# Distance attention worked in pairs of head groups, with three distance buffers and its loads on the sync engine

## What is computed

```python
q2 = jnp.sum(q * q, axis=-1)
k2 = jnp.sum(k * k, axis=-1)
qk = jnp.einsum('bhid,bhjd->bhij', q, k)
d2 = jnp.maximum(q2[..., :, None] + k2[..., None, :] - 2.0 * qk, 1e-12)
attn = jax.nn.softmax(-jnp.sqrt(d2), axis=-1)
out = jnp.einsum('bhij,bhjd->bhid', attn, v)
out = out.transpose(0, 2, 1, 3).reshape(B, N, D)
return out @ wo.T + bo
```

## Time and profile before

| what | us |
|---|---|
| median of 3 runs | 3940.42 (3935.94 to 3940.86) |
| the profiled execution's own time | 3938.66 |
| its span, first to last instruction | 3937.0 |
| the stage of the change: first minimum starts | 3236.41 |
| PE, DVE, ACT, POOL busy over the span | 3315.0, 3175.2, 2294.0, 1649.5 |

### The profile page before, as it was taken

The page is one execution under the profiler, slowest core; times in us unless marked ns, Lnnn a source line. Parts: engine busy times, 40 slices in busy tenths (PEclk is TensorE's granted clock), DMA queues, the critical chain, the costliest instruction groups (busy, mean ns, idle before and its releaser), DMA issues. The chain is left out here.

```text
span 3937.0 us, 57222 instructions
## 1 busy us (share of the span) xinstructions
PE 3315.0 (84%) x16738; PEld 1754.3 (45%) x16738; DVE 3175.2 (81%) x5041; ACT 2294.0 (58%) x2742; POOL 1649.5 (42%) x781
## 2 busy tenths in 40 slices
PE   6758888888879997869799999799996977777776
PEld 3322333333327775645333343599986651112111
DVE  6869999999978887747589886487767768888887
ACT  4767666666652225624266666222222758999998
POOL 0009998989971110012100000000015328899996
PEclk9879999999989998978799999899998987888888
DMA  3553333333213356837623321221113553344342
GB/s 123 197 195 127 121 119 139 140 140 140 103 48 109 98 163 159 209 91 255 207 68 75 80 69 57 80 64 53 43 33 112 175 161 93 114 119 127 117 122 87
DMA packets 294390, 465.45 MB, mean 118 GB/s; under 512 B 40711, under 2 KB 237960, under 8 KB 273790
## 3 DMA queue, kind: packets, MB, share of 16 engines
q1 hardware_dynamic: 249838, 412.98, 32.7%
q10 hardware_dynamic: 44432, 51.10, 4.9%
HBM read 322.44 MB, written 141.33 MB: 118 GB/s over the span
## 5 line engine op out<-in xcount | busy, mean ns | idle before, releaser
L1170 PE MATMUL mamba_psum<-mamba_hc,scan_ident 128*128 128x512 f32 x1024 | 550.2, 645 | 88.6 <-DVE mamba_hc L1078 70.7
L3584 POOL TENSOR_TENSOR distance_dist<-distance_dist,distance_least_all 128x2048 f32<-128x2048 f32 x124 | 559.1, 4541 | 78.1 <-DMA distance_least_all<-distance_least_rows 78.1
L3079 POOL TENSOR_TENSOR scatter_out<-scatter_out,scatter_s 128x512 f32<-128x512 f32 x16 | 31.2, 1959 | 1019.6 <-ACT scatter_out L3096 997.6
L1101 DVE TENSOR_TENSOR_SCAN mamba_psum<-mamba_psum,mamba_drive 128x512 f32<-128x512 f32 x352 | 415.2, 1218 | 22.7 <-issue 10.5
L2657 DVE TENSOR_REDUCE causal_row_max<-causal_psum 128x1 f32<-128x512 f32 x512 | 333.2, 683 | 77.4 <-PE causal_psum L2727 67.5
L1170 PEld LDWEIGHTS mamba_psum<-mamba_hc,scan_ident 128*128 128x128 f32 x1024 | 176.3, 195 | 417.5 <-DVE mamba_hc L1078 253.1
L2616 ACT ACTIVATE causal_probs<-causal_psum 128x1024 f32<-128x1024 f32 x256 | 250.6, 1021 | 121.9 <-PE causal_psum L2750 121.7
L3760 PE MATMUL distance_psum<-distance_shared_k_stacks,distance_shared_q_stacks 102*128 102x512 bf16 x512 | 211.6, 509 | 115.2 <-DVE distance_least L3678 56.2
L3678 DVE TENSOR_REDUCE distance_least<-distance_psum 128x2 f32<-128x1024 f32 x256 | 294.5, 1217 | 9.6 <-PE distance_psum L3760 9.4
L3714 DVE TENSOR_SCALAR distance_dist<-distance_psum 128x1024 f32<-128x1024 f32 x192 | 227.1, 1221 | 82.0 <-PE distance_psum L3775 82.0
L1021 POOL TENSOR_TENSOR mamba_drive<-scan_u,scan_b_all 128x1024 f32<-128x1024 f32 x64 | 149.7, 2351 | 289.6 <-POOLq L31 289.6
(11 more groups left out here) (466 smaller groups left out, 8758.1 us busy)
## 6 DMA issues: line engine op xcount, KB each, us to landing
distance_least_all<-distance_least_rows SPq DMA_DIRECT2D x32, 1024.0 KB, 4.6
scan_b_all<-bc SPq DMA_DIRECT2D x16, 1024.0 KB, 4.5
scan_c_all<-bc SPq DMA_DIRECT2D x16, 1024.0 KB, 6.7
mamba_b_all<-bc SPq DMA_DIRECT2D x16, 1024.0 KB, 4.9
mamba_c_all<-bc SPq DMA_DIRECT2D x16, 1024.0 KB, 7.4
choice_w<-L_ffn_w SPq DMA_DIRECT2D x16, 1024.0 KB, 5.1
z<-mamba_in_z SPq DMA_DIRECT2D x8, 1024.0 KB, 3.9
xc<-mamba_in_xc SPq DMA_DIRECT2D x8, 1024.0 KB, 3.9
```

Of the source, the lines that this page charges most:

```text
L1101: dve.tensor_tensor_scan(out, bank, drive[:, n % DRIVES], 0.0, ALU.mult, ALU.add).then_inc(h_ready, 1)
L1170: pe.matmul(ps[:, Y_BANK + m % 2], ident[:, :], hc[:, n % PRODUCTS], start=False, stop=(s == DS - 1)).then_inc(y_summed, 1)
L3584: pool.tensor_tensor(dist[:, g % 2, kt], dist[:, g % 2, kt], least_all[:, g % 2], ALU.subtract).then_inc(shifted, 1)
```

## The change

The step is now over a pair of groups (n and n+1 of one batch), 16 pairs in all, 7 of them with a projection of the batch before (`projected`).

- ACT: the roots of the minima of both groups in one go (128x32), ahead of all else of the step; then units 0 and 1 of the first group, the copy, three roots of the first group, the second group's units 0 and 1, and the other five roots. Then the four exponentials of the second group of the pair before, and the four of the first group of this pair.
- DVE, PE: all 16 units of second scores of a pair, then all 16 units of first scores of the next pair. The turn of a pair's first group lies between the clamps (L3714's work), that of its second in the minima of the next step, after 13 of 16. The projection is made in two halves within the second scores of the second group.
- The three score buffers now serve strictly in turn, and the distances have three buffers in SBUF.
- One store of the minima and two spreading loads per pair. SP issues all loads that ACT issued.
- The weights of the stage lie on the other side of SBUF, so that the experts' buffers are given back before the stage begins; the barrier of that stands ahead of the stage and no longer behind it.

The core of the diff; left out are the helpers and most of what is removed (PAIRS is 16, LOOP_PAIRS is 6):

```diff
+class GroupPair:
+    def __init__(self, b, half, index):
+        self.b, self.half, self.index = b, half, index
+        self.groups = [(b, 2 * half + k) for k in range(2)]
+        self.odd = half == 1
+    def n(self, k):
+        return self.b * NG + 2 * self.half + k
+    def slot(self, k):
+        return (2 * self.index + k) % 3
...
+def group_pairs(eng, step):
+    for p in range(2):
+        step(GroupPair(0, p, p))
+    with eng.Fori(0, 2) as i:
+        for j in range(LOOP_PAIRS):
+            step(GroupPair(i * (LOOP_PAIRS // 2) + 1 + j // 2, j % 2, 2 + j))
+    for p in range(2 + 2 * LOOP_PAIRS, PAIRS):
+        step(GroupPair(p // 2, p % 2, p))
...
-        dist = c.sb("dist", [P, 2, TT, GH * T])
+        dist = c.sb("dist", [P, 3, TT, GH * T])
...
+        def wait_buffer(pe, pair, unit):
+            if unit < BUFFERS:
+                pe.wait_ge(a_min, pair.n(1) * UNITS + (7, 8, 6)[unit])
+                return
+            before = unit - BUFFERS
+            k, u = divmod(before, UNITS)
+            if k >= 2:
+                pe.wait_ge(a_min, (pair.n(0) + k) * UNITS + u + 1)
+            elif u < ACT_UNITS:
+                pe.wait_ge(above_floor, pair.n(k) * ACT_UNITS + u + 1)
+            else:
+                pe.wait_ge(clamped, pair.n(k) * DVE_UNITS + u - ACT_UNITS + 1)
...
+                def spread_least(pair):
+                    p = pair.b * 2 + pair.half
+                    sp.wait_ge(least_copied, p + 1)
+                    sp.dma_start(least_dram, least_t[:, :]).then_inc(least_stored, DMA)
+                    sp.wait_ge(least_stored, (p + 1) * DMA)
+                    for k in range(2):
+                        sp.wait_ge(shifted, pair.n(k) * TT + TT)
+                        rows = least_dram[k * GH * TT:(k + 1) * GH * TT]
+                        sp.dma_start(least_all[:, k], rows.rearrange("n q -> (n q)").partition_broadcast(P)).then_inc(
+                            least_loaded[k], DMA)
...
+                def load_v(n, b, g):
+                    if isinstance(b, int) and b == NB - 1:
+                        return
+                    sp.wait_ge(pv_done, n * TT + TT + PV_SET)
+                    attention.load_v(sp, v_in, b + 1, g)
+                def step(pair):
+                    spread_least(pair)
+                    if projected(pair):
+                        sp.wait_ge(xo_ready, (pair.b - 1) * 2 + 2)
+                        sp.dma_start(gate[:, :, :], token_tiles(gate_in, pair.b - 1)).then_inc(gx_loaded, DMA)
+                        sp.dma_start(x[:, :, :], token_tiles(x_in, pair.b - 1)).then_inc(gx_loaded, DMA)
+                    if not is_start(pair):
+                        before = pair.other(-1)
+                        load_v(before.n(0), *before.groups[0])
+                    if not (isinstance(pair.b, int) and pair.b == NB - 1):
+                        sp.wait_ge(s_done, pair.n(1) * UNITS + UNITS)
+                        for b, g in pair.groups:
+                            load_side(sp, b + 1, g, False)
+                            load_side(sp, b + 1, g, True)
+                    if not is_start(pair) and not is_last(pair):
+                        before = pair.other(-1)
+                        load_v(before.n(1), *before.groups[1])
+                    if projected(pair):
+                        sp.wait_ge(xo_ready, (pair.b - 1) * 2 + 4)
+                        sp.dma_start(token_tiles(x_out, pair.b - 1), xo[:, :, :]).then_inc(xo_stored, DMA)
...
+                def step(pair):
+                    shift(pair, 0)
+                    if projected(pair):
+                        b = pair.b - 1
                         pool.wait_ge(gx_loaded, b * 2 * DMA + 2 * DMA)
                         for j in range(2):
                             tiles = slice(2 * j, 2 * j + 2)
...
                             tiles = slice(2 * j, 2 * j + 2)
                             pool.wait_ge(gated, b * 2 + j + 1)
                             pool.tensor_tensor(xo[:, tiles], xo[:, tiles], x[:, tiles], ALU.add).then_inc(xo_ready, 1)
-                run(pool, step)
+                    if not is_last(pair):
+                        shift(pair, 1)
...
+                def step(pair):
+                    p = pair.b * 2 + pair.half
+                    act.wait_ge(a_min, pair.n(1) * UNITS + UNITS)
+                    act.activation(least[:, :, :], least[:, :, :], ACT.Relu, bias=minus_floor[:, 0:1]).then_inc(least_clamped, 1)
+                    act.wait_ge(least_clamped, p + 1)
+                    act.activation(least[:, :, :], least[:, :, :], ACT.Sqrt, bias=floor[:, 0:1]).then_inc(least_ready, 1)
+                    floor_scores(pair, 0, 0)
+                    floor_scores(pair, 0, 1)
+                    act.wait_ge(least_turned, p + 1)
+                    for loaded in least_loaded:
+                        wait_past(act, loaded, p * DMA)
+                    act.copy(least_t[:, :], ps[0:2 * GH * TT, 7, 0:P]).then_inc(least_copied, 1)
+                    for kt in range(3):
+                        root(pair, 0, kt)
+                    floor_scores(pair, 1, 0)
+                    floor_scores(pair, 1, 1)
+                    root(pair, 0, 3)
+                    for kt in range(TT):
+                        root(pair, 1, kt)
+                    if not is_start(pair):
+                        before = pair.other(-1)
                         for kt in range(TT):
-                            if kt == 0:
-                                act.wait_ge(above_floor, (n + 1) * ACT_UNITS)
-                                act.activation(dist[:, g % 2, kt], dist[:, g % 2, kt], ACT.Sqrt, bias=floor[:, 0:1]).then_inc(sqrt_ready, 1)
-                            else:
-                                act.wait_ge(clamped, n * DVE_UNITS + 2 * kt + 2 - ACT_UNITS + 2)
-                                act.activation(dist[:, g % 2, kt], dist[:, g % 2, kt], ACT.Sqrt).then_inc(sqrt_ready, 1)
-                    if out is not None:
-                        b, g = out
-                        for kt in range(TT):
-                            if is_last(out):
-                                act.wait_ge(last_shifted, kt + 1)
-                            else:
-                                act.wait_ge(shifted, (b * NG + g) * TT + kt + 1 + 2 * TT)
-                            act.activation(dist[:, g % 2, kt], dist[:, g % 2, kt], ACT.Exp, scale=-1.0).then_inc(p_ready, 1)
-                            if is_last(out) and kt == 0:
-                                load_gx(NB - 1)
+                            power(before.n(1), before.slot(1), kt)
+                    for kt in range(TT):
+                        power(pair.n(0), pair.slot(0), kt)
...
+                def step(pair):
+                    before = None if is_start(pair) else pair.other(-1)
+                    after = None if is_last(pair) else pair.other(1)
+                    clamp(pair, 0, range(2, 6))
                     if before is not None:
-                        b, g = before
-                        dve.wait_ge(pv_done, (b * NG + g) * TT + 3 * TT)
-                        context.turn(dve, b * NG + g, ps[:, 6])
-                        context.scale_in(dve, b, g, ps[:, 6])
-                    if first is not None:
-                        minima(*first)
-                    if before is not None and g % 2 == 1:
-                        if g == 1 and not (isinstance(b, int) and b == 0):
-                            dve.wait_ge(proj_done, b * 4)
-                        context.turn_back(dve, b * NG + g, g)
-                    if is_last(mid):
-                        shift_last()
-                    if proj is not None and not isinstance(proj, int):
-                        add_bias(proj, 1)
-                    elif proj is not None:
-                        finish_last(0)
-                        finish_last(1)
-                minima(0, 0)
+                        turn(before.n(0), *before.groups[0])
+                    clamp(pair, 0, range(6, 8))
+                    clamp(pair, 1, range(2, 6))
+                    if projected(pair):
+                        add_bias(pair.b - 1, 0)
+                    clamp(pair, 1, range(6, 8))
+                    if projected(pair):
+                        add_bias(pair.b - 1, 1)
+                    if after is not None:
+                        minima(after, 0, range(8))
+                        minima(after, 1, range(5))
+                    else:
+                        for kt in range(3):
+                            shift_last(pair, kt)
+                    if before is not None:
+                        turn(before.n(1), *before.groups[1])
+                        turn_back(before.n(1), *before.groups[1])
+                    if after is not None:
+                        minima(after, 1, range(5, 8))
+                    else:
+                        shift_last(pair, 3)
...
+                def step(pair):
```

(39 more changed lines are left out.)

336 lines of the change are left out of this document (161 added, 175 removed).

## The result

The changed kernel takes 3997.0 us (median of 4 runs, 3986.4 to 3998.7), the kernel before 3939.5 beside it: ratio 1.0142, 95% interval 1.0123 to 1.0161. It is slower by 57 us, outside the predicted range of 3905 to 3978.

The account below looks back on a forecast made before the run. The prediction took ACT, 95% busy, as the present bound and DVE's chain as the next. Steps summing to 643.5 plus a last step of 62.4 gave 705.9 us, 5.3 above 700.6, so 3946 us, range 3905 to 3978.

Parts of the forecast that it names:

- Table loads and floors: Table loads fall from 31 + 31 to 16 + 16; floors per pair: ACT 36.8 us, POOL 38.6, DVE 35.9.
- DVE's chain is the bound now: In the new order DVE's waits and work set the pace, 42.1 us a mean pair; ACT idles 2.5 and more.
- the named minimum: L3678's minimum at the roots of the minima: ACT predicted to wait there and at the copy, some 4 us a pair.
- The walk without projection: Step-by-step timing of one pair from a step's last minimum: next zero at 40.44 us (39.83 at full clock); 40.9 taken.
- the slow clock to the head: Unit 1, unit 2 and the output at a step's start may be slow: up to 1.0 us, 0.5 taken.
- the price of PE's clock with a projection: An idle 2 us of PE before the projection may make it slow: up to 1.8 us, 0.75 taken; 43.6 a pair.
- the prediction's own signs of being wrong: No ACT wait at the step's head, no POOL idle, or PE's clock far from 0.82; two steps expected at 84 us.
- First step and last step: Stage ends: first step about 36.1 us without outputs and turns; last step, from second scores to the end, 62.4.
- The sum: Stage from its first minimum to the span's end: 643.5 + 62.4 = 705.9 us, 5.3 more than 700.6.
- POOL, SP and the moved loads: POOL hidden, waiting under 5 us a pair for its load; SP has 13 us slack; moving loads from ACT wins nothing.
- half clock at head and projection: Rival: PE gaps make it slow at both, 41.4 and 45.1 a pair, 3958; upper form 43.2 and 46.9, 3983; chance 0.23.
- ACT stays the bound: Rival: ACT sets the pace and the table-load gain comes through, down to POOL's 38.6 a pair, 3888; chance 0.17.

Follow-up runs that it names:

- run 1: Changed kernel plus unread matmuls where PE stood idle, and four score units of a projected step computed twice: 3947.65 us, ratio 1.0029.
- Run 2: Changed kernel with the projection moved in four parts from the clamps into the first scores, biases among the minima: 3950.1 us, ratio 1.0041.
- Run 12: Kernel before, with the loads of q, k, v, gate and x issued from the sync engine instead of ACT: 3934.2 us, ratio 1.0000.
- Runs 4: Kernel before, with the exponential replaced by the identity, leaving one of 62 table loads; exponentials not computed: 3921.4 us, ratio 0.9959.
- run 6: Changed kernel, with the exponential replaced by the identity, so one table load remains; exponentials not computed: 3970.9 us, ratio 1.0092.

## Why the prediction was wrong

By its own steps:

- **Table loads and floors**: right. 16 + 16 loads, and ACT has 36.6 and 36.9 busy in the two kinds of pair (36.8 said).
- **"DVE's chain is the bound now"**: right, if PE's units that DVE waits for are counted in, as the walk did. ACT waits 102.4 us at the named minimum, DVE 110.2 for PE, and run 1 shortens the stage through PE alone.
- **The walk without projection**: the order of events held. Unit 3 at 3.7 (3.64), clamp 4 at 5.3 (5.06), turn at 7.6 (7.3), unit 10 at 12.7 (11.74), minima 19.4 (18.5), minimum 7 at 28.5 (28.15). At high clock the step is 40.3 (39.83). It missed that the second output is also at half clock, which holds up minimum 8 by 1.61, and the wait of PE for bank 6. It also gave the slow clock to the head, which is at full clock in these steps. 42.7 came, 40.9 was taken, 8 x 1.8 = 14 us.
- **The step that failed is the price of PE's clock with a projection**, "up to 1.8, of which I take 0.75". The projection's first half was taken at 1.8 us with a part of the price on top, and the second at full clock. Both took 3.6 to 3.8, and each is waited for by a clamp: unit 10 came at 15.7 in place of 12.79, the minima at 27.3 in place of 22.2. So 49.0, not 43.6: 6 x 5.4 = 32 us. A row of full clock from the old order, where the projection stood in a busy stretch of PE, was carried to a place where PE has just been idle. Run 1 confirms the term: with the first half at full clock (1.89) and the second partly (3.11), the step is 44.5. Run 2 confirms it from the other side: with the projection off the clamps, no step is above 44.2. Two of the prediction's own signs of being wrong were there: a clock of 0.76 in place of 0.82, and 92.1 us for two steps in place of 84.
- **First step and last step**: 37.7 for 36.1, and 65.9 for 62.4; 1.6 and 3.5 us. The 3.5 of the last step are the same term once more: its second scores and biases end at 25.6 in place of 22.2, and from there on all is as long as walked.
- **The sum**: 14 + 32 + 1.6 + 3.5 = 51, which is 757.1 (from the first minimum at 3239.68 to the end of the span) less 705.9. The start of the stage, 3.3 us later than before, is not of the change: it lies between 3230 and 3244 in the profiled executions, with no order by kernel.
- **POOL, SP and the moved loads**: right in what they cost. Run 12 shows the loads at nothing, and the exponentials wait 0.8 us for POOL. POOL's own wait is 134.9/16 = 8.4 us a pair where under 5 was said, since the step outlasts its work by more.
- **The rivals**: "half clock at head and projection" in its upper form, 43.2 and 46.9 for 3983, came nearest, and half of its mechanism is what came: the projection was slow, and dearer still. The head was not: in most steps the clock is 1.00 there, with the output of tile 3 at 1.06 and unit 4 at 0.60. That its 43.2 is near the 42.7 is luck; the loss there lies at the second output. It was given 0.23, and its projection half belonged in the forecast. "ACT stays the bound" is excluded by ACT's 102.4 us of waits at the last minimum. Runs 4 and 6 agree: without 61 loads the old order gains 16 us, and without 31 the new one is still at 3971, not at 3888.

What stays open: whether run 6 gained more than the 19 us that lie on the chain, which its spread does not tell; and what decides whether a gap of PE has half or full clock behind it, since gaps of 1.9 to 2.1 us had both.

## What to carry to other kernels

When a change moves work, the others' waits become gaps of PE, and the matmuls that follow can be at half clock. Here they were behind 20 of 40 gaps of 1.5 us and more. So carry no row of full clock to a place behind a new gap: price matmuls on which the next engine waits at both levels, and take the slow one as likely as the fast one, not a part of it. Better still, place them where nobody waits, as run 2 did. Before regrouping to save table loads, run the kernel once without them: that one run bounds what fewer loads give that order (here 16 us). And where PE has gaps, matmuls that nobody reads are a cheap test, and sometimes a cure.

## What the runs showed of the hardware

A subtraction of two operands in SBUF takes DVE 2.40 us alone. While POOL does such work it takes 4.35 on average, and POOL's gate operations slow down from 1.26 to 3.3 us at the same time. In the last step of the changed kernel, first DVE and then POOL:

```profile
3956.49 13.05 DVE L3769 TENSOR_TENSOR distance_dist<-distance_dist,distance_least_all 128x2048 f32<-128x2048 f32 x3
...
3971.65 2.40 DVE L3769 TENSOR_TENSOR distance_dist<-distance_dist,distance_least_all 128x2048 f32<-128x2048 f32 x1
```

```profile
3942.84 17.97 POOL L3642 TENSOR_TENSOR distance_dist<-distance_dist,distance_least_all 128x2048 f32<-128x2048 f32 x4 [6.92 <-DMA distance_least_all<-distance_least_rows]
3960.77 6.61 POOL L3652 TENSOR_TENSOR distance_xo<-distance_xo,distance_gate 128x512 f32<-128x512 f32 x2
```

DVE's three take 6.47, 3.37 and 3.37. POOL's last subtraction, which began first, is not slowed (17.97 for four, has 18.05). DVE's first ends 2.15 us after it, which is about one subtraction alone. From there on the two engines seem to take turns: POOL's first gate operation ends 1.1 us after DVE's subtraction, and DVE's next 2.2 after that. In the kernel before they met only for 0.8 us, where DVE's first subtraction took 2.97 and the other three 2.28. Other DVE work beside POOL's subtractions (clamps, minima: 1.13 from start to start) shows no such loss. In the changed kernel it cost nothing: ACT's twelve last exponentials follow one another without a wait while it lasts. The Trainium skill (GPSIMD Engine Reference, Specifications) names contention of the two engines where DVE has two SBUF inputs; the trace agrees and gives it this price.

Also unexpected was how much more work could go into PE for less time: the trace of run 1 has some 390 matmuls more than that of the changed kernel, and PE is busy 3350.8 us in it against 3365.1.
